# A two-layer recurrent block on one core: TensorE's passes within a head put in another order, and one score tile computed from halves

## What is computed

```
kv = ss @ w_kv ; keys, values = split(kv)
grads = grad over (mem_w0, mem_w1) of  sum(mean((silu(k @ w0) @ w1 - v)^2) * lr)    per chunk
momentum = scan(gm, -grads) ; updates = scan(1 - decay, momentum)                   over chunks
x    = q @ (mem_w0 + updates[0])
vals = silu(x) @ (mem_w1 + updates[1])
out  = (rmsnorm(vals) * gamma * gate) @ w_combine
```

## Time and profile before

| | |
|---|---|
| median of 3 runs | 1265.42 us (1263.39 to 1266.05) |
| span of the profiled execution | 1264.6 us |
| TensorE busy | 1127.4 us, 89% |
| VectorE, ScalarE, GpSimd busy | 741.5, 682.3, 589.8 us (59%, 54%, 47%) |

### The profile page before, as it was taken

The page is one execution under the profiler, slowest core; times in us unless marked ns, Lnnn a source line. Parts: engine busy times, 40 slices in busy tenths (PEclk is TensorE's granted clock), DMA queues, the critical chain, the costliest instruction groups (busy, mean ns, idle before and its releaser), DMA issues. The chain is left out here.

```text
span 1264.6 us, 21008 instructions
## 1 busy us (share of the span) xinstructions
PE 1127.4 (89%) x6645; PEld 922.8 (73%) x6646; DVE 741.5 (59%) x1913; ACT 682.3 (54%) x1355; POOL 589.8 (47%) x568
## 2 busy tenths in 40 slices
PE   4689746999999999999999999999999999968980
PEld 3356534888888888888888888888888888858980
DVE  4488856656655555555556555565555566545546
ACT  4567523555555555555555555555555555534541
POOL 2166752777544444444444444444444444433553
PEclk9688857999999999999999999999999999998995
DMA  9033204000000000000000000000000000004434
GB/s 197 28 91 93 83 25 144 20 22 18 17 1 1 2 7 0 0 7 0 0 0 7 0 0 0 7 0 0 7 0 0 0 7 1 2 8 128 142 96 133
DMA packets 65604, 40.92 MB, mean 32 GB/s; under 512 B 4300, under 2 KB 61974, under 8 KB 65431
## 3 DMA queue, kind: packets, MB, share of 16 engines
q1 hardware_dynamic: 57783, 31.30, 9.5%
q0 software_dynamic: 2304, 4.74, 1.2%
q10 hardware_dynamic: 5472, 4.33, 1.0%
HBM read 22.49 MB, written 15.77 MB: 30 GB/s over the span
## 5 line engine op out<-in xcount | busy, mean ns | idle before, releaser
L1022 DVE TENSOR_TENSOR p_sb<-bank,cf 128x512 f32<-128x512 f32 (+3 forms) x512 | 218.8, 480 | 1.0 <-PE bank L877 1.0
L1104 POOL TENSOR_TENSOR qa_low<-qa,qa_high 128x450 fp32r<-128x450 f32 x64 | 94.4, 1475 | 119.1 <-ACT qa_high L986 119.1
L1112 POOL TENSOR_TENSOR rs<-ms,neg_half 128x4 f32<-128x4 f32 x64 | 84.7, 1324 | 128.6 <-DVE ms L1032 128.6
L1031 DVE TENSOR_SCALAR ms<-bank 128x3 f32<-128x3 f32 x64 | 10.3, 161 | 213.4 <-PE bank L959 213.4
L900 PE MATMUL bank<-p_sb,du_t 128*128 128x450 f32 (+3 forms) x512 | 132.0, 401 | 0.0
L1128 POOL TENSOR_TENSOR sq_rest<-sq,sq_high 128x450 f32<-128x450 f32 x64 | 67.1, 1048 | 135.0 <-ACT sq_high L999 135.0
L900 PE MATMUL bank<-p_sb,err_t 128*128 128x450 f32 (+3 forms) x512 | 128.8, 394 | 0.4 <-DVE p_sb L1022 0.4
L900 PEld LDWEIGHTS bank<-p_sb,du_t 128*128 128x128 f32 x512 | 82.0, 190 | 44.7 <-issue 32.7
L900 PEld LDWEIGHTS bank<-p_sb,err_t 128*128 128x128 f32 x512 | 87.1, 190 | 37.0 <-issue 23.6
L1050 DVE SCALAR_TENSOR_TENSOR acc<-bank,rg,acc 128x128 f32<-128x128 f32 x224 | 62.7, 344 | 71.6 <-POOL rg L1116 71.6
L1132 POOL TENSOR_TENSOR sq_low<-sq_rest,sq_mid 128x450 bf16<-128x450 f32 x64 | 66.4, 1038 | 75.4 <-ACT sq_mid L1007 75.3
(11 more groups left out here) (295 smaller groups left out, 3204.4 us busy)
## 6 DMA issues: line engine op xcount, KB each, us to landing
x<-in_L_attn_inputs SPq DMA_DIRECT2D x16, 256.0 KB, 3.0
rows<-sorted_rows SPq DMA_DIRECT2D x40, 64.5 KB
sorted_rows<-xl_all SPq DMA_DIRECT2D x1, 2064.0 KB, 18.6
x_rows<-x SPq DMA_DIRECT2D x8, 256.0 KB, 2.4
xn_rows<-xn SPq DMA_DIRECT2D x8, 256.0 KB, 2.4
xl_all<-xl SPq DMA_DIRECT2D x8, 256.0 KB, 3.3
ew<-in_L_ffn_w SPq DMA_DIRECT2D x8, 256.0 KB, 4.3
xn_all<-xn_rows SPq DMA_DIRECT2D x8, 256.0 KB
```

The lines of the kernel that those rows point to most:

```text
L1022: last = nc.vector.tensor_tensor(dst, src, w, ALU.mult)
L1104: nc.gpsimd.tensor_tensor(parts[1][:], whole[:], parts[0][:], ALU.subtract).then_inc(done, 1)
L1112: nc.gpsimd.tensor_tensor(rs[:], ms[:], m.neg_half[:, 0:T], ALU.pow).then_inc(g_rs, 1)
```

## The change

Score tile 2 (194 columns) is now made from halves, like tiles 0 and 1 (`SC_SPLIT`), so that `yk` holds 384 columns and `yb` 128. Only tile 3 (66 columns) is plain. The tiles are taken in the order 0, 1, 2, 3 everywhere, and tile 3 moves from bank 5 to bank 6, beside tile 2. The third signal of a score group is now given behind tile 3 and not behind tile 2.

TensorE's order in `step` becomes: U and EB, scores of `s` tiles 0, 1, 2, product into VB, QA, product into EB; then, plain, score tile 3 of `s`, `apply` to VB, the transposes of `err`; then from halves the product into U, scores of `f` tiles 0, 1, 2, `project` XB; then, plain, the transposes of `du`, score tile 3 of `f`, `apply` to XB, `w_out` and the sums. On ScalarE the copy of `err_t` moves ahead of the cast `sq_high`.

```diff
-SC_BANK = [4, 5, 6, 5]
-SC_COL = [0, 0, 0, 384]
+SC_BANK = [4, 5, 6, 6]
+SC_COL = [0, 0, 0, 256]
-SC_ORDER = [0, 1, 3, 2]
+SC_ORDER = [0, 1, 2, 3]
+SC_SPLIT = [0, 1, 2]
...
-        yb = sb("yb", [P, S - 2 * P])
-        yk = pair("yk", [P, 2 * P])
+        yb = sb("yb", [P, S - 3 * P])
+        yk = pair("yk", [P, 3 * P])
...
-                        if i < 2:
+                        if i in SC_SPLIT:
...
-                        if i != 1:
+                        if i != 2:
                             last.then_inc(done, 1)
...
-                            pe.wait_ge(made, SC_BANKS * n + {0: 1, 1: 2, 2: 3}[i])
+                            pe.wait_ge(made, SC_BANKS * n + i + 1)
...
-                        scores(s_2[s[1] % 2], xs_2, s_sb[s[1] % 2][:, 2 * P:], xs, p_s1)
+                        scores(s_2[s[1] % 2], xs_2, None, None, p_s1, SC_SPLIT)
+                        pe.wait_ge(v_ms, k)
+                        product(VB[:, 0:QW], [w[:] for w in w1], [part[:] for part in xs_2])
...
                     if s is not None:
-                        pe.wait_ge(v_ms, k)
+                        scores(None, None, s_sb[s[1] % 2][:, len(SC_SPLIT) * P:], xs, p_s1, plain)
                         pe.wait_ge(a_et, k + 1)
-                        product(VB[:, 0:QW], [w[:] for w in w1], [part[:] for part in xs_2])
                         apply(VB, err_t, v_p1, k).then_inc(p_v, 1)
...
-                        scores(yk, qa_2, yb, qa, p_s0, SC_ORDER[:-1])
+                        scores(yk, qa_2, None, None, p_s0, SC_SPLIT)
+                        pe.wait_ge(a_et, n + 1)
+                        project(XB, m.w_x, f, SHIFT)
                         pe.wait_ge(v_du, n + 1)
                         for t in range(T):
                             last = pe.transpose(EB[:, t * P:t * P + P], du[:, t * P:t * P + P], m.ident[:])
                         last.then_inc(p_dt, 1)
-                        scores(yk, qa_2, yb, qa, p_s0, SC_ORDER[-1:])
-                        pe.wait_ge(a_et, n + 1)
-                        project(XB, m.w_x, f, SHIFT)
+                        scores(None, None, yb, qa, p_s0, plain)
...
+                    if f is not None:
+                        act.wait_ge(p_et, n + 1)
+                        nc.scalar.copy(err_t[:].rearrange("p t d -> p (t d)"), XB[:]).then_inc(a_et, 1)
+                    if s is not None:
                         act.wait_ge(a_sq, k + 1)
                         nc.scalar.copy(sq_3[0][:], sq[:]).then_inc(a_hi, 1)
                     if f is not None:
-                        act.wait_ge(p_et, n + 1)
-                        nc.scalar.copy(err_t[:].rearrange("p t d -> p (t d)"), XB[:]).then_inc(a_et, 1)
```

More of the change, by code:

```diff
@@ L883, in project, with scores @@
                     return product(out[:, 0:width], [part[:, at[1], :] for part in w], y, stop=stop)
-                def scores(left_2, right_2, left, right, done, tiles=SC_ORDER):
+                def scores(left_2, right_2, left, right, done, tiles):
                     for i in tiles:
                         out = m.bank[SC_BANK[i]][:, SC_COL[i]:SC_COL[i] + QW - P * i]
-                        if i < 2:
+                        if i in SC_SPLIT:
                             last = product(out, [part[:, i * P:i * P + P] for part in left_2], [part[:, P * i:] for part in right_2])
                         else:
-                            last = pe.matmul(out, left[:, (i - 2) * P:(i - 1) * P], right[:, P * i:], start=True, stop=True)
-                        if i != 1:
+                            last = pe.matmul(out, left[:, (i - len(SC_SPLIT)) * P:(i - len(SC_SPLIT) + 1) * P], right[:, P * i:], start=True, stop=True)
+                        if i != 2:
                             last.then_inc(done, 1)
@@ L904, in step @@
                 def step(f, s, z):
+                    plain = SC_ORDER[len(SC_SPLIT):]
                     if f is not None:
@@ L1020, in weigh @@
                         if i != 3:
-                            dve.wait_ge(made, SC_BANKS * n + {0: 1, 1: 2, 2: 3}[i])
+                            dve.wait_ge(made, SC_BANKS * n + i + 1)
                         last = nc.vector.tensor_tensor(dst, src, w, ALU.mult)
-                        if i != 1:
+                        if i != 2:
                             last.then_inc(done, 1)
@@ L1059, in step @@
                             high, low = (part[:, bass.ds(f[0], 1), 0:S].rearrange("p a n -> p (a n)") for part in m.y_all)
-                            nc.vector.tensor_copy(yk[0][:], high[:, 0:2 * P]).then_inc(v_y, 1)
-                            nc.vector.tensor_copy(yk[1][:], low[:, 0:2 * P]).then_inc(v_y, 1)
-                            nc.vector.tensor_tensor(yb[:], high[:, 2 * P:], low[:, 2 * P:], ALU.add).then_inc(v_y, 1)
+                            nc.vector.tensor_copy(yk[0][:], high[:, 0:3 * P]).then_inc(v_y, 1)
+                            nc.vector.tensor_copy(yk[1][:], low[:, 0:3 * P]).then_inc(v_y, 1)
+                            nc.vector.tensor_tensor(yb[:], high[:, 3 * P:], low[:, 3 * P:], ALU.add).then_inc(v_y, 1)
                         if h == 0:
```

## The result

The changed kernel takes 1343.24 us (median of 4 runs, 1339.01 to 1348.39), the kernel before 1265.74 (the three runs given above and a fourth): a ratio of 1.0611 (95% interval 1.0588 to 1.0634). The forecast was 1322 us, slower with a chance of 0.92, and a range of 1285 to 1405. The spans of the two profiled executions are 1337.0 and 1264.6 us. The attention itself, from the start of the first head to that of the last, takes 983.2 us against 908.1; the preparation, which the change doesn't touch, happened to end 4.0 us earlier in the profile of the changed kernel (195.8 against 199.8). Over all the profiles of this case it ended between 194.2 and 200.7.

What follows compares the result with a forecast made beforehand. TensorE bound the kernel, 13.65 of 14.41 us a head; 64 heads by 0.84 (53.8), plus 4.8 for first heads, minus 1, gave 57.6 on 1264.6, with 0.8 outside: 1323, stated as 1322; range 1285 to 1405.

Steps and rivals of the forecast that it cites:

- The narrow passes: Score tile 2's three passes of 194 columns: 0.11 us each, 0.33 for the three, as the plain tile.
- The dear passes: Rival, chance 0.30: 194-column passes cost 0.33 us each, 1.28 us more by 64 heads, 1404 us.
- passes of 0.16: Milder case of costly 194-column passes: 0.16 us each, 0.26 by 64, 17 us more, 1339 us.
- The first half: Step up to the `err` product: QA no earlier, product 0.12 us later, wait for `err_low` 0.82 in place of 0.26.
- the exclusion: VectorE and GpSimd lock their shared SBUF port pair against each other; without it the sum is some 10 us lower.
- The second half: From the `err` product on: a wait of 0.84 us for `du_t` ahead of the second `apply`.
- the handover of 1.12: From the last `du` transpose's start to the stream of the second `apply`, through ScalarE's copy `du_t`: 1.12 us.
- The ordinary head: One head's length: 15.25 us, 0.84 more than 14.41; 64 heads give 53.8 us.
- The 0.05 that the forecast took off the second `apply`: Second `apply` takes 1.80 us, as no 66-column record stands ahead of a longer one; plain work saved 0.05.
- the first heads: First head of a sequence, seven times: VectorE's extra instructions delay the `err` product, 7 by 0.68, 4.8 us extra.
- Each opening costs: Rival: each opening of a run of halves behind plain work costs 0.14 us; two of four go, 1304 us.
- Not slower: Rival, chance 0.06: `err_low` is ready before TensorE, so the 0.82 wait vanishes; 1270, or 1264 us, no change.

Runs made afterwards that it cites:

- halves_only: Kernel before the change with score tile 2 made from three passes of halves, nothing moved: 1266.57 us, 0.9997 of the kernel before.
- first_back: Changed kernel with only score tile 3 of head `s` put back right behind tile 2: 1318.61 us, 1.0403 of the kernel before the change.
- second_back: Changed kernel with the second half's order undone, transposes of `du` ahead of tile 3 and XB again: 1294.85 us, 1.0219 of the kernel before.
- copies_early: Changed kernel with the casts and sum of `y` moved to the end of the sequence before: 1328.24 us, 1.0492 of the kernel before the change.
- copies_away: Changed kernel with `y` casts and sum moved to the sequence before, and the `cf` copy moved to right ahead of its weighing: 1320.87 us, 1.0437.
- both_err_first: Changed kernel with tile 3 of `s` and the second half's order put back, plus ScalarE's cast `qa_high` moved behind `err_high`: 1262.78 us, 0.9975.
- after_err_first: Changed kernel with ScalarE's cast `qa_high` moved behind `err_high`: 1374.43 us, 1.0849 of the kernel before the change.

## Why the prediction was right, and where it fell short

**The narrow passes.** 0.11 us each, as taken from the records of 66 columns: measured 0.09, 0.11, 0.11. The dear passes, the rival with 0.30, didn't come; halves_only shows it on the time as well. The measured 1343 us by themselves would not have told: they lie 1 us above the forecast's own range of 1302 to 1342, and nearer to the 1339 that the prediction gives for passes of 0.16. It is the rows that decide.

**The first half.** QA starts no earlier, since `acc` is no earlier: right (the EB product 4.13 after the head's start, 4.11 before). The weighing resumes 5.19 after it (5.17 forecast), `err_low` ends at 7.91 (7.92), the product streams at 8.06 (8.09), with a wait of 0.79 (0.82). That the signal behind tile 3 is what holds VectorE is shown by first_back: the 0.77 us in the weighing are gone there. The forecast said that this half loses only 0.12 us; it is 0.09. Its remark that without the exclusion the sum would be some 10 us lower is too small: L1072 ends 0.24 earlier then, by 64 that is 15.

**The second half.** A wait of 0.84, as forecast; second_back takes away 0.63 of it; the rest, some 0.2, is the handover of 1.12 less the 0.89 of cover.

**The ordinary head.** 15.28 against 15.25. The small remainder is in `w_out`: 1.27 and not 1.21 us from its start to the head's end, as its first record now stands behind one of 66 columns. The 0.05 that the forecast took off the second `apply` come back there.

**The mis-sized term** is the first heads, 4.8 us extra in the sum. From the first head's start to the last's, the attention takes 75.1 us more, where the forecast has 56.8 (57.6 less the 0.84 of the last head). The seven first heads grew by 24.6 in all and not by 10.6; that is 14 of the 18 us missing. The very first head of all grew by 1.9 and not by 0.84, which no run explains, and the other 55 by 0.885 each. In the first heads of sequences two things were left out. The casts of `y` were counted at their own length, though they now start together with `qa_low`, and the exclusion that the forecast applied to L1077 holds for them too (0.9 us; copies_early and copies_away show it, the one by moving the victim to the next copy, the other by having none). And the wait for `err_low` was priced as only itself, when five times of seven, at an idle time of 2.2 us, the half clock came behind it as well (1.6 us each). Which pauses bring it and which don't stays open: the same pause of 2.2 in two first heads of this kernel and in all seven of second_back brought none, and a pause of 1.5 in copies_early none.

**The other rivals.** "Each opening costs" would have given time back in the changed kernel (1304 us). second_back and first_back have an opening more each, and their ordinary heads, 14.65 and 15.20, are no longer than expected without a price for it (14.67 and 15.28). "Not slower" would have needed `err_low` before TensorE. No variant with the product into VB ahead of QA had that: the nearest is both_err_first, where TensorE waits some 0.1 for it and the head is 14.24; in the changed order the same move made `err_low` later.

## What to carry to other kernels

Before gathering an engine's work into longer runs of one kind, write down for each handover what stands between the release and its use; what is moved out of that gap comes back as a wait, here 0.77 us of 0.94 us of cover. When a signal moves later in one engine's order, everything queued behind its waiter moves too, however unrelated it is: here the weighing of a tile that nobody needed yet held up a subtraction that TensorE did need. What that costs is not the wait that the profile shows but what an edit gives back: 0.09 us in an ordinary head, where the next chain was as long, and 1.5 to 3.1 us in the first heads, where it pushed casts onto GpSimd's operation. And where VectorE and GpSimd both work on operands in SBUF, a third engine can decide by the order in which it hands them their input who runs first: one edit on ScalarE gained 0.7% in one kernel and lost 2.3% in another.

## What the hardware showed

- A cast or copy with a single SBUF input was held up by a GpSimd subtraction just as the operations with two inputs were (L1077 0.87 against 0.69, `err_low` 1.62 against 0.69): 1.24 against 0.35 us (128 x 384 cast), 0.96 against 0.28 (128 x 256 copy). VectorE's weighing and L1075, which read one operand from PSUM and one from SBUF, ran beside `qa_low` at their usual 0.62 and 0.68. The Trainium skill (SBUF — State Buffer, "SBUF: two separate sides") names both kinds of operation, two SBUF inputs or a 2-port mode, as those that take the shared pair. The runs agree for two SBUF inputs; in which mode the casts and the copy ran no run shows.
- A GpSimd operation that was waiting got its turn between two VectorE instructions issued back to back: after_err_first, `qa_low` started 0.34 us ahead of L1077's end and took 1.33 us (1.15 unhindered), and `err_low` behind L1077 took 1.62.
- The granted clock fell to half for 3.4 us in five first heads of the changed kernel, 0.4 to 1.5 us after TensorE had resumed from an idle time of 2.2 us (1.1 in the head shown, and full again from 581.7 on); in two with the same idle time it didn't fall. Before the change it was at half for the attention's first 5 us, until 205.0, and at full from there to the attention's end; the 1.00 of the earlier trace rows is rounded.
